# A fused attention-pooling and per-sample linear kernel: one bias row in four is loaded by DMA and added by VectorE, the count product moves to GpSimd, and the start-up order is rewritten

## What is computed

```python
attn   = tanh(x @ W1 + b1)                 # 128 x 128
scores = attn @ v                          # one score for each row
mask   = prefix, postfix or all-but-self, by the sample's type id
p      = softmax(where(mask, scores, -1e30))
y      = x + (p @ x) / count(mask)         # 128 x 512
out    = y + y @ W[cat] + b[cat]           # W has 64 matrices of 512 x 512
```

## Time and profile before

| | |
|---|---|
| time, median of 3 runs | 323.19 us (321.76 to 323.3) |
| time of the profiled execution | 322.09 us |
| its span | 320.3 us |
| mean granted TensorE clock | 0.994 |
| busy: TensorE, VectorE, ScalarE, GpSimd | 311.7, 283.8, 274.4, 3.6 us |
| DMA moved | 101.49 MB, mean 317 GB/s |

### The profile page before, as it was taken

The page is one execution under the profiler, slowest core; times in us unless marked ns, Lnnn a source line. Parts: engine busy times, 40 slices in busy tenths (PEclk is TensorE's granted clock), DMA queues, the critical chain, the costliest instruction groups (busy, mean ns, idle before and its releaser), DMA issues.

```text
span 320.3 us, 4751 instructions
## 1 busy us (share of the span) xinstructions
PE 311.7 (97%) x1374; PEld 242.3 (76%) x1374; DVE 283.8 (89%) x300; ACT 274.4 (86%) x447; POOL 3.6 (1%) x17
## 2 busy tenths in 40 slices
PE   8999897999999999999999999999999999999996
PEld 4445675878888887887888788888878888787884
DVE  3558799999999999999999999999999999999950
ACT  2376988979989899998989999898998989899852
POOL 3010000000000000000000000000000000000000
PEclk9999997999999999999999999999999999999999
DMA  7999999899989989998999999898899989974123
GB/s 227 429 356 422 421 382 335 303 354 308 356 308 345 353 300 381 303 376 299 358 322 320 351 328 368 313 350 317 307 405 297 360 311 353 334 282 178 37 96 131
DMA packets 21290, 101.49 MB, mean 317 GB/s; under 512 B 2385, under 2 KB 2386, under 8 KB 11282
## 3 DMA queue, kind: packets, MB, share of 16 engines
q1 hardware_dynamic: 20882, 100.15, 85.2%
q10 hardware_dynamic: 288, 0.79, 0.7%
q0 software_dynamic: 96, 0.26, 0.3%
HBM read 84.41 MB, written 16.78 MB: 316 GB/s over the span
## 4 chain that ended last, share of the span: by engine, by line
PE 91%; ACT 3%; DVE 2%; DMA 2%; issue 1%; SPq 0%; DVEq 0%; ACTq 0%
PE ps_y L564 17%; PE ps_y L565 16%; PE ps_y L566 16%; PE ps_pre L520 11%; PE ps_y L579 4%; PE ps_y L552 4%; PE ps_y L576 4%; PE ps_y L577 4%; PE ps_y L578 4%; PE ps_pre L509 2%; PE ps_pT L543 2%; DMA x_raw<-in_x 2%; PE ps_scores L530 1%; DVE w_lo L378 1%; PE ps_scores L532 1%; ACT w_hi L261 1%
## 5 line engine op out<-in xcount | busy, mean ns | idle before, releaser
L378 DVE TENSOR_TENSOR w_lo<-w_raw,w_hi 128x2048 fp32r<-128x2048 f32 x60 | 137.1, 2285 | 4.0 <-ACT w_hi L261 4.0
L261 ACT ACTIVATE w_hi<-w_raw 128x2048 fp32r<-128x2048 f32 x60 | 115.9, 1933 | 1.5 <-DVE w_raw L366 1.5
L564 PE MATMUL ps_y<-w_hi,xT_hi 128*128 128x512 f32 x240 | 96.6, 403 | 0.3 <-DVE w_lo L378 0.3
L566 PE MATMUL ps_y<-w_hi,xT_lo 128*128 128x512 f32 x240 | 94.4, 394 | 0.0
L565 PE MATMUL ps_y<-w_lo,xT_hi 128*128 128x512 f32 x240 | 94.4, 393 | 0.0
L566 PEld LDWEIGHTS ps_y<-w_hi,xT_lo 128*128 128x128 f32 x240 | 45.3, 189 | 10.0
L564 PEld LDWEIGHTS ps_y<-w_hi,xT_hi 128*128 128x128 f32 x240 | 45.4, 189 | 9.6 <-ACT out_sb L303 0.5
L565 PEld LDWEIGHTS ps_y<-w_lo,xT_hi 128*128 128x128 f32 x240 | 45.4, 189 | 9.3
L405 DVE TENSOR_TENSOR z_lo<-ps_y,z_hi 128x512 fp32r<-128x512 f32 x64 | 43.5, 682 | 6.3 <-ACT z_hi L297 6.3
L297 ACT ACTIVATE z_hi<-ps_y 128x512 fp32r<-128x512 f32 x64 | 39.0, 610 | 9.3 <-PE ps_y L566 4.8
L366 DVE TENSOR_TENSOR w_raw<-w_raw,ident 128x512 f32<-128x512 f32 x63 | 42.8, 681 | 0.6 <-DMA w_raw<-in_L_cond_W 0.6
(11 more groups left out here) (71 smaller groups left out, 284.5 us busy)
## 6 DMA issues: line engine op xcount, KB each, us to landing
w_raw<-in_L_cond_W SPq DMA_DIRECT2D x63, 1024.0 KB, 8.3
out<-out_sb SPq DMA_DIRECT2D x64, 256.0 KB, 5.4
x_raw<-in_x SPq DMA_DIRECT2D x15, 1024.0 KB, 7.1
w_raw<-in_L_cond_W SPq DMA_DIRECT2D x2, 512.0 KB, 6.6
x_raw<-in_x ACTq DMA_DIRECT2D x1, 512.0 KB, 5.9
x_raw<-in_x SPq DMA_DIRECT2D x1, 512.0 KB, 5.2
w_pack<-in_W_b_v ACTq DMA_DIRECT2D x1, 257.0 KB, 3.2
b_raw<-in_L_cond_b POOLq DMA_DIRECT2D x2, 128.0 KB, 7.2
```

What stands on the lines that cost most here:

```text
L261: nc.scalar.activation(w_hi[k % NH][:], w_raw[k % NW][:], ACT.Copy).then_inc(w_hi_ready, 1)
L378: nc.vector.tensor_tensor(w_lo[k % NL][:], w_raw[k % NW][:], w_hi[k % NH][:].bitcast(F32), ALU.subtract).then_inc(w_lo_ready, 1)
L564: nc.tensor.matmul(y[:], xT_hi[q][:, c, xs], w_hi[k % NH][:, c, :], start=(c == 0), stop=False)
L566: last = nc.tensor.matmul(y[:], xT_lo[q][:, c, xs], w_hi[k % NH][:, c, :], start=False, stop=(c == DC - 1))
```

## The change

Of each group the second sample (k % 4 == 1, `WIDE`) gets its bias in another way. A DMA spreads the bias row `b[cat]` over the 128 partitions of `out_sb[1]` (`load_wide`). `pz` leaves out its fourth matmul for that sample, VectorE adds the bank to `out_sb[1]` in place (`add_wide`, in the loop at b = 0 behind `split_z_lo`), and ScalarE has no `copy_out` for it. The count product of `row_scale_group` goes to GpSimd. At the start x of group 0 and the weights of sample 0 come in one DMA each in place of two halves, the weights issued by ScalarE's queue and the ids too; the two `b_raw` loads go from GpSimd's queue to SyncE's, behind the weights of sample 4; TensorE's second warm-up has 7 matmuls in place of 11. In the prologue's written orders the high split of w 4 goes ahead of `tanh_group(1)`, `exp_group(1)` goes ahead of z_hi 3, `tanh_group(2)` ahead of the split of w 8, `split_av_lo` 1 and 2 go behind w_lo 4 and ahead of w_lo 8; the loops start one or two iterations later. In the loops themselves only the points named above change.

```diff
-            return k + 2
+            return k + 1
+        def wide(k):
+            return k % G == WIDE
+        def wait_out(engine, k):
+            if wide(k):
+                engine.wait_ge(sum_ready, k // G + 1)
+            else:
+                engine.wait_ge(out_ready, k - (k + G - WIDE - 1) // G + 1)
...
             def store(k):
-                sp.wait_ge(out_ready, k + 1)
+                wait_out(sp, k)
...
-            sp.dma_start(ids_row[:], ids.rearrange("(a n) -> a n", a=1)).then_inc(ids_in, 16)
-            sp.dma_start(x_raw[0][:, halves[0], :], xg[0][:, halves[0], :]).then_inc(x0_in[0], 16)
+            def load_wide(g):
+                cat = sp.value_load(ids_row[0:1, G * g + WIDE:G * g + WIDE + 1], min_val=0, max_val=C - 1)
+                if g >= 1:
+                    sp.wait_ge(out_stored[WIDE], 16 * g)
+                sp.dma_start(out_sb[WIDE][:], bias[bass.ds(cat, 1), :].to_broadcast([P, D])).then_inc(wide_in, 16)
+            load_x(0)
             sp.wait_ge(ids_in, 16)
-            cat_0 = sp.value_load(ids_row[0:1, 0:1], min_val=0, max_val=C - 1)
-            for h, c in enumerate(halves):
-                sp.dma_start(w_raw[0][:, c, :], w[bass.ds(cat_0, 1), :, c, :].rearrange("a p c h -> p (a c) h"))\
-                    .then_inc(w0_in[h], 16)
...
             load_w(4)
+            sp.dma_start(b_raw[0:C, :], bias).then_inc(b_low_in, 16)
+            sp.dma_start(b_raw[C:P, :], bias).then_inc(b_high_in, 16)
...
             load_w(6)
+            load_wide(0)
...
                     load_x(g + 3)
+                if b == 2 and 1 <= g < GROUPS:
+                    load_wide(g)
...
                 .then_inc(consts_ready, 1)
-            pool.wait_ge(w_in[2], 16)
-            pool.dma_start(b_raw[0:C, :], bias).then_inc(b_low_in, 16)
-            pool.dma_start(b_raw[C:P, :], bias).then_inc(b_high_in, 16)
+            pool.wait_ge(seen_ready, 1)
+            for g in range(GROUPS):
+                pool.wait_ge(exp_ready, g + 1)
+                if g >= 1:
+                    pool.wait_ge(scale_ready, g)
+                nc.gpsimd.tensor_tensor(row_div[:], row_sum[:], seen[:, G * g:G * (g + 1)], ALU.mult)\
+                    .then_inc(div_ready, 1)
...
             def split_xT_hi(g):
-                act.wait_ge(x_in[g % NX], 16 * (g // NX + (1 if g % NX else 0)))
+                act.wait_ge(x_in[g % NX], 16 * (g // NX + 1))
...
+            act.dma_start(ids_row[:], ids.rearrange("(a n) -> a n", a=1)).then_inc(ids_in, 16)
             act.dma_start(w1_pack[:], w1).then_inc(w1_in, 16)
-            act.dma_start(x_raw[0][:, halves[1], :], xg[0][:, halves[1], :]).then_inc(x0_in[1], 16)
+            act.wait_ge(ids_in, 16)
+            cat_0 = act.value_load(ids_row[0:1, 0:1], min_val=0, max_val=C - 1)
+            act.dma_start(w_raw[0][:], w[bass.ds(cat_0, 1)].rearrange("a p c h -> p (a c) h")).then_inc(w_in[0], 16)
...
             nc.scalar.activation(b_both[:], b_raw[:], ACT.Copy).then_inc(b_hi_ready, 1)
+            split_w_hi(4)
             tanh_group(1)
-            split_w_hi(4)
-            split_z_hi(3)
...
             exp_group(1)
+            split_z_hi(3)
...
             scale_group(1)
-            copy_out(1)
...
             split_w_hi(6)
+            split_z_hi(4)
+            split_mix_hi(1)
...
-            for k in range(G + 1, B + 3):
+            copy_out(2)
+            split_z_hi(5)
+            tanh_group(2)
+            split_w_hi(8)
+            copy_out(3)
+            split_w_hi(9)
+            for k in range(G + 3, B + 3):
...
                     exp_group(g + 1)
-                copy_out(k - 3)
+                if not wide(k - 3):
+                    copy_out(k - 3)
...
-            def add_identity_0(h):
-                dve.wait_ge(w0_in[h], 16)
-                blocks = diagonal(0)[:, h * HALF:(h + 1) * HALF, :]
-                nc.vector.tensor_tensor(blocks, blocks, eye.to_broadcast([P, HALF, P]), ALU.add).then_inc(wi_ready, 1)
             def add_identity(k):
-                dve.wait_ge(w_in[k % NW], 16 * (k // NW + (1 if k % NW else 0)))
+                dve.wait_ge(w_in[k % NW], 16 * (k // NW + 1))
...
             def row_scale_group(g):
-                dve.wait_ge(exp_ready, g + 1)
-                nc.vector.tensor_tensor(row_div[:], row_sum[:], seen[:, G * g:G * (g + 1)], ALU.mult)\
-                    .then_inc(div_ready, 1)
...
+            def add_wide(g):
+                k = G * g + WIDE
+                dve.wait_ge(pz_done, k + 1)
+                dve.wait_ge(wide_in, 16 * (g + 1))
+                nc.vector.tensor_tensor(out_sb[WIDE][:], ps_y[k % NY][:], out_sb[WIDE][:], ALU.add)\
+                    .then_inc(sum_ready, 1)
...
                 .then_inc(setup_step, 1)
-            add_identity_0(0)
-            add_identity_0(1)
...
                 .then_inc(setup_step, 1)
-            split_av_lo(0)
...
                                            ALU.is_equal, ALU.add).then_inc(bias_ready, 1)
+            add_identity(0)
+            split_av_lo(0)
...
             add_identity(2)
-            dve.wait_ge(seen_ready, 1)
...
                 .then_inc(bias_ready, 1)
+            split_w_lo(4)
...
             add_identity(5)
-            split_w_lo(4)
             max_group(1)
+            split_w_lo(5)
+            row_scale_group(1)
...
             split_z_lo(3)
-            row_scale_group(1)
-            split_w_lo(5)
...
             add_identity(7)
+            add_wide(0)
...
             split_w_lo(7)
+            split_av_lo(2)
...
-            for k in range(G + 2, B + 1):
+            split_z_lo(5)
+            split_w_lo(8)
+            add_identity(10)
+            for k in range(G + 3, B + 1):
...
                 split_z_lo(k - 1)
+                if b == 0:
+                    add_wide(g - 1)
...
                 for c in range(DC):
-                    if k == 0 and c % HALF == 0:
-                        pe.wait_ge(wi_ready, c // HALF + 1)
-                    elif k >= 1 and c == 0:
+                    if c == 0:
...
                 if k >= NY:
-                    pe.wait_ge(out_ready, k - NY + 1)
+                    wait_out(pe, k - NY)
...
                 nc.tensor.matmul(y[:], ml, z_hi[k % NZ][:], start=False, stop=False, skip_group_check=True)
-                nc.tensor.matmul(y[:], mh, z_lo[k % NZ][:], start=False, stop=False, skip_group_check=True)
+                last = nc.tensor.matmul(y[:], mh, z_lo[k % NZ][:], start=False, stop=wide(k), skip_group_check=True)
+                if wide(k):
+                    last.then_inc(pz_done, 1)
+                    return
...
                 .then_inc(ids_spread, 1)
-            warm_up(11)
+            warm_up(7)
```

More of the change, by code:

```diff
@@ L39, in program @@
     assert A == P and w1.shape[1] == DC * A + 2 and D == DC * P and C == P // 2
-    HALF = DC // 2
     NX, NT, NW, NH, NL, NZ, NO, NY = 3, 2, 5, 4, 3, 3, 4, 5
+    WIDE = 1
+    assert NO == G
     RAW = G
@@ L116, in program @@
         b_high_in = sem("b_high_in")
-        x0_in = [sem(f"x0_in{h}") for h in range(2)]
-        w0_in = [sem(f"w0_in{h}") for h in range(2)]
         x_in = [sem(f"x_in{i}") for i in range(NX)]
@@ L157, in program @@
         out_ready = sem("out_ready")
+        sum_ready = sem("sum_ready")
+        wide_in = sem("wide_in")
         block = ctx.enter_context(nc.Block())
-        halves = [slice(h * HALF, (h + 1) * HALF) for h in range(2)]
         def w_count(k):
@@ L504, in hidden_raw @@
                     pe.wait_ge(attn_ready, g)
-                    pe.wait_ge(x_in[g], 16)
+                pe.wait_ge(x_in[g], 16)
                 for c in range(DC):
-                    if g == 0 and c % HALF == 0:
-                        pe.wait_ge(x0_in[c // HALF], 16)
                     last = nc.tensor.matmul(ps_pre[:], w1_pack[:, c * A:(c + 1) * A], x_raw[g][:, c, :],
```

## The result

The change made the kernel slower by 0.6%: 323.65 us median of 20 runs (323.32 to 325.07) against 321.87 us of 20 runs before (320.54 to 323.3), ratio 1.0058 with a 95% interval of 1.0044 to 1.0072. The bound that the prediction set, 0.5%, lies within the interval. The profiled execution took 324.01 us with a span of 321.9; before it was 322.09 and 320.3.

What follows compares the result with a forecast made beforehand. A closed VectorE-ScalarE path of 18.76 us a group was taken to bound the kernel, TensorE only just held. Start -0.2, twelve turns +0.9, end -0.46: together +0.2 us, so 323.4 us from the 323.19 median; range 318.7 to 325.4.

Steps and rivals of the forecast that it cites:

- the ring: Steady part: closed VectorE-ScalarE path from one group's maximum to the next, without TensorE; 18.76 us, forecast 18.83, +0.075 a group.
- M: Start of VectorE's maximum in a group, numbered by group; times within a turn are counted from it.
- the sum's slot: VectorE's time for add_wide, between z_lo and the identity: 0.60 us taken, bounds 0.48 and 0.69.
- GpSimd's product at no cost: Steady part: count product on GpSimd ends before VectorE's reciprocal wants it at M + 4.0; cost 0, hidden even at 1.5 us.
- The spread row in time: Steady part: bias row's DMA lands before add_wide wants it, some 9.7 us after issue; cost 0, cover 1.4 us or more.
- The start: Before the second group's maximum: xw_raw(0) at about 11.2 us, +1.2 (bounds 0 and +2.8); M(2) at 52.6, 0.5 later.
- M(3): Start of the maximum at 71.67 us before, where the twelve counted turns begin; forecast 71.4, -0.2 us.
- The catch of the slow clock: M(2) to M(3): TensorE's idling and 0.50 clock at 51 to 52 us, and VectorE's 0.73 us wait, would go.
- The end: After the last scores_group: TensorE runs free and has two of the removed matmuls there, -0.46 us.
- Throughput as the bound: Rival, steady part: fullest engine's work sets the period, 18.5 us; gain 3.7 us, 319.5 us; chance 0.24.
- The start as the costly rival: Rival: x and w 0 land past +2.8, or idle TensorE starts at lower clock; +2.5 us and more, 325.9; chance 0.08.
- The other two: Rivals, steady part: GpSimd's product delays the reciprocal, 329 us, chance 0.06; spread row lands late, 338, chance 0.04.

Runs made afterwards that it cites:

- Matmuls back: Changed kernel with the removed bias matmul of the WIDE samples put back, so their bias is added twice; 324.39 us, ratio 1.0066 to the kernel before.
- product back: Changed kernel with the count product back on VectorE and GpSimd idle; 323.65 us, ratio 1.0042 to the kernel before.
- work moved along VectorE's order alone: Changed kernel treating each group's first sample, sum at b = 3: 322.26 us, ratio 1.0002; that kernel with the reciprocal ahead of the sum: 319.55 us, 0.9922.
- the five products: Changed kernel with five count products on GpSimd in each group in place of one, four to a spare tile; 324.71 us, ratio 1.0077 to the kernel before.
- w 0 first with 11 warm-up matmuls: Changed kernel with w 0 whole on SyncE's queue ahead of w 1 and 11 warm-up matmuls in place of 7; 321.34 us, ratio 0.9979.
- the old loads alone: Changed kernel with the first loads (x and w 0 in halves, SyncE's queue) and 11 warm-up matmuls of before; 321.69 us, ratio 0.9991.
- the old loads with the reciprocal first: Changed kernel treating each group's first sample, sum at b = 3 behind the reciprocal, first loads and warm-up of before; 317.43 us, ratio 0.9864.

## Why the prediction was right, and where it was off

- *What bounds the kernel.* Right. Matmuls back, product back: the period stays at 18.8; work moved along VectorE's order alone: it falls to 18.68 and 18.44. A chain that is 91% TensorE said otherwise; the waits said it rightly.
- *The new length of the ring.* Right, for each part: 18.83 forecast, 18.82 measured, xT_lo at M + 8.56 forecast and 8.55 measured, the sum's slot 0.60, the wait for `w_hi` 0.36 forecast and 0.38 measured. Twelve turns cost 0.80 us, forecast 0.9. One of the signs that it named was off: ScalarE's wait for the maximum was to grow by some 0.5 us and grew by 0.16; the rest of its free time went into the new wait of 0.51 us for TensorE's hidden product, which is not on the ring.
- *GpSimd's product at no cost.* Right in the steady part: the product ends at M + 2.9, and five of them at M + 3.55, ahead of M + 4.0. *The spread row in time:* right, no wait for it shows.
- *The start.* The mechanism was right and the size off: the step that failed is the term "+1.2 us" for `xw_raw(0)`. It was +2.8, the upper end of the range given for it, and M(3) came 1.2 us later than before where -0.2 was forecast. I had taken the landing of the second half as that of the whole, and counted the sharing with w 1 only as a bound. That the bound held is in part luck: its 1.7 us is what half of w 0's 1.05 MB takes at 317 GB/s, and half the bandwidth for all of it would be 3.3 us more; measured were 12.0 - 10.4 = 1.6. A row was also told the wrong way round: w 4's DMA was not in by 24.56, VectorE was free from then on and waited for it until 24.94; the sum used 24.56 only for when VectorE is free, so it stands. From there on the worked order held: from `xw_raw(0)` to M(2) I had 52.6 - 11.2 = 41.4, measured 41.2. That the shorter warm-up costs nothing was right in this kernel for the wrong reason: not because it ended before x came, but because w 0 came later still.
- *The catch of the slow clock.* Right in the result: M(2) to M(3) is 18.82 in place of 19.58, TensorE has no stop at 48 to 51 us, and its granted clock stays at 1.00 there. But the order of the prologue did not do it alone. The run without WIDE samples has the same order and the clock at 1.00 too, and VectorE still waits 0.50 us for the scores; that part went with the WIDE samples. TensorE does stand idle later, 1.45 us up to 60.23, with the clock still shown as 1.00.
- *The end.* -0.46 forecast, -0.4 measured.
- *The sum.* +0.2 us forecast, +1.6 in the spans, +0.58% in the medians. 323.4 us against 323.65 looks closer than it is: the median of three runs that it started from was 1.3 us above that of the twenty. The move was likeliest to be too small to tell (0.55) and came out just over that bound.
- *The rivals.* Throughput as the bound is refuted for this order, and is what holds once the order leaves VectorE no wait. The start as the costly rival came half true: costlier than forecast, but within its bounds. Its lower clock shows in one run, the five products: `hidden_raw(0)` took 3.70 us there, TensorE then stood idle 2.2 us for w 0, and the granted clock was 0.50 (1.2 GHz) from 13 to 15 us. The other two did not occur.

## What to carry to other kernels

Where two engines wait only for each other, once a group, add up the closed path before pricing what is removed: work taken off an engine that isn't on it is free already, and work moved onto it is paid in full every turn. Put added work in front of an instruction that waits anyway, behind whatever another engine is waiting for; find all paths through the place, not only the one that is longest now. At the start, issue the transfer that is needed first ahead of the next one and not beside it.

## What the runs showed of the hardware

- *GpSimd's small product ends with VectorE's large subtraction.* GpSimd's timeline in the kernel after:

```profile
19.60 0.20 POOL L269 TENSOR_TENSOR row_div<-row_sum,seen 128x4 f32<-128x4 f32 x1 [16.41 <-ACT probs L299]
36.68 0.91 POOL L269 TENSOR_TENSOR row_div<-row_sum,seen 128x4 f32<-128x4 f32 x1 [16.88 <-ACT probs L299]
...
75.14 0.64 POOL L269 TENSOR_TENSOR row_div<-row_sum,seen 128x4 f32<-128x4 f32 x1 [18.17 <-ACT probs L299]
```

VectorE computes w_lo while the second and third run, and nothing while the first does. With no w_lo running the product takes 0.20 us. The one at 75.14 ends at 75.78, 0.05 us after the w_lo that started at 73.45 and took 2.28; the one at 36.68 ends at 37.59, 0.06 us after the w_lo of 35.24 to 37.53. Whether it starts earlier or later in a w_lo, the product ends just behind it. That is what the Trainium skill (SBUF — State Buffer, § Who interferes with whom) states, that a VectorE instruction with two SBUF inputs and a GpSimd one that reads SBUF hold each other up for the whole first instruction; the trace agrees. Here the wait was hidden; no run took the overlap away by itself.

- *The first matmuls ran at two speeds.* `hidden_raw(0)`, eight matmuls, took 3.7 to 3.9 us in the profiles of five kernels (before, w 0 first with 11 warm-up matmuls, the old loads alone, the old loads with the reciprocal first, the five products) and 5.3 to 6.7 us in the other nine, with most of the matmuls 0.85 us apart in place of 0.43. The granted clock is shown as 1.00, the level of 2.4 GHz, all the while, as in the kernel after, by stretch of 1 us (the matmuls in each are 2; in the kernel before they were 4):

```profile
7.00:8.00 1.00, 1.00 (x2) 0.33 (x1) 0.96 (x3) 0.00 (x0) 0.00 (x0) 1.00 1.07 442
8.00:9.00 1.00, 1.00 (x2) 0.33 (x1) 0.59 (x3) 0.00 (x0) 0.00 (x0) 1.00 0.98 410
```

With 7 warm-up matmuls it was slow in seven of eight profiles, with 11 in two of six. The two runs with w 0 first, 1.0028 with 7 and 0.9979 with 11, suggest that more of them help; what decides in a single execution stays open.
